# Two-layer decoder, cross attention: a ring of seven PSUM banks for the transposed scores, the denominators in one of its banks, and a semaphore of their own for them

## The reference, cut to what matters

```python
x = x + _L0_xattn_ref(_layernorm(x), ctx_1024, ctx_1024, ..., mask_SxS2_bk1, mask_BxS2_bf0)
...
q = (query @ Wq + bq).reshape(B, Sq, H, hd)
k = (key @ Wk + bk).reshape(B, Sk, H, hd)
v = (value @ Wv + bv).reshape(B, Sk, H, hd)
score = jnp.einsum('bqhd,bkhd->bhqk', q, k)
score = jnp.where(cmask, -jnp.inf, score)
att = jax.nn.softmax(score * scale, axis=-1)
ret = jnp.einsum('bhqk,bkhd->bqhd', att, v).reshape(B, Sq, D)
return ret @ Wo + bo
```

## Time and profile before

| | us |
|---|---|
| median of 3 runs | 1632.97 (1627.45 to 1636.53) |
| the profiled execution, device time | 1634.7 |
| its span, first to last instruction | 1632.8 |
| PE busy | 1401.2 (86%) |
| DVE busy | 1015.4 (62%) |
| ACT busy | 758.5 (46%) |
| share of the chain that ended last | PE 72%, DVE 14%, ACT 3% |
| mean granted TensorE clock | 0.921 of 2.4 GHz |

### The profile page before, as it was taken

One profiled execution on the slowest core, in us unless ns is written; L12 is line 12 of the kernel. 1 busy time (PEld: TensorE's weight loads), 2 busy tenths in 40 slices (PEclk: granted clock), 3 DMA queues, 4 the chain that ended last, 5 costly groups with the idle time before them and its releaser, 6 DMA issues.

```text
span 1632.8 us, 44292 instructions
## 1 busy us (share of the span) xinstructions
PE 1401.2 (86%) x17837; PEld 872.8 (53%) x17837; DVE 1015.4 (62%) x2607; ACT 758.5 (46%) x1942; POOL 236.9 (15%) x216
## 2 busy tenths in 40 slices
PE   5888888696499999999967989898989998889856
PEld 3343443393267676766643466445654565346545
DVE  3566656424477777877744677667766776777633
ACT  1313142251266666666632277235734474337534
POOL 2011121123030030110001200011001200030035
PEclk8989899797799999999987999899998999799969
DMA  9600000023230100100023000000000000000031
GB/s 320 244 16 0 16 1 7 17 60 99 77 144 4 24 22 10 36 3 16 4 55 69 1 1 2 3 14 1 2 3 14 1 2 1 1 14 2 1 88 53
DMA packets 56617, 59.09 MB, mean 36 GB/s; under 512 B 27853, under 2 KB 42064, under 8 KB 55264
## 3 DMA queue, kind: packets, MB, share of 16 engines
q1 hardware_dynamic: 53600, 50.97, 9.9%
q0 software_dynamic: 2528, 5.27, 1.0%
q10 hardware_dynamic: 288, 0.03, 0.0%
HBM read 32.56 MB, written 24.14 MB: 35 GB/s over the span
## 4 chain that ended last, share of the span: by engine, by line
PE 72%; DVE 14%; issue 4%; ACT 3%; SPq 2%; DMA 2%; POOL 2%; ACTq 0%; POOLq 0%; DVEq 0%
PE ps L1163 7%; PE ps L1551 6%; PE ps L1570 5%; PE ps L264 5%; PE ps L1143 4%; PE ps L1584 4%; PE ps L1153 4%; PE ps L1184 4%; DVE arena L610 4%; PE ps L1539 3%; PE ps L485 3%; PE ps L509 3%; PE ps L1198 2%; PE ps L1593 2%; PE ps L834 2%
## 5 line engine op out<-in xcount | busy, mean ns | idle before, releaser
L1296 DVE TENSOR_REDUCE nmax<-ps 128x1 f32<-128x512 f32 x256 | 166.7, 683 | 60.6 <-PE ps L1153 59.8
L1626 ACT ACTIVATE arena<-ps,arena 128x512 f32<-128x512 f32 (+3 forms) x256 | 135.3, 531 | 116.4 <-DVE arena L1689 109.2
L1689 DVE TENSOR_REDUCE arena<-ps 128x1 f32<-128x512 f32 (+3 forms) x256 | 124.3, 487 | 74.2 <-PE ps L1555 72.4
L1256 ACT ACTIVATE arena<-ps,nmax 128x512 f32<-128x512 f32 x172 | 118.8, 691 | 83.8 <-DVE nmax L1296 82.5
L1570 PE MATMUL ps<-sqc,arena 128*128 128x128 f32 x640 | 107.6, 290 | 20.3 <-DVE arena L1697 20.1
L1304 DVE COPY arena<-ps 128x512 f32<-128x512 f32 x128 | 88.0, 687 | 35.4 <-PE ps L1163 33.8
L264 PE MATMUL ps<-identb 128*128 128x512 bf16 x366 | 105.9, 453 | 1.4 <-DVE kcol L742 1.4
L610 DVE TENSOR_REDUCE arena<-ps 128x8 f32<-128x1232 f32 x64 | 89.0, 1437 | 29.1 <-PE ps L473 29.1
L1697 DVE TENSOR_SCALAR arena<-arena 128x512 f32<-128x512 f32 (+3 forms) x256 | 100.9, 394 | 9.1
L1551 PE MATMUL ps<-arena 64*128 64x384 f32 (+3 forms) x512 | 105.4, 490 | 0.0
L1584 PE MATMUL ps<-arena 128*64 128x128 f32 x1280 | 98.2, 284 | 0.0
(11 more groups left out here) (355 smaller groups left out, 2661.9 us busy)
## 6 DMA issues: line engine op xcount, KB each, us to landing
xs_d<-onehot SPq DMA_DIRECT2D x4, 2560.0 KB, 26.9
cw<-in_cw SPq DMA_DIRECT2D x2, 2048.0 KB, 11.0
rv<-in_rv SPq DMA_DIRECT2D x2, 1536.0 KB, 17.4
late<-in_gw SPq DMA_DIRECT2D x3, 1024.0 KB, 9.7
arena<-gs_d SPq DMA_DIRECT2D x23, 129.0 KB
onehot<-q_s SPq DMA_DIRECT2D x96, 8.0 KB
arena<-xs_d SPq DMA_DIRECT2D x23, 64.0 KB
xs_d<-arena SPq DMA_DIRECT2D x23, 64.0 KB, 1.6
```

What stands on the lines that cost most here:

```text
L1256: nc.scalar.activation(PB[k % 6], ps[:, k % 5, :], ACT.Exp, bias=nmax[:, u:u + 1], accum_out=rsum[:, b % 2, u:u + 1]).then_inc(SD["exp"], 1)
L1296: nc.vector.tensor_reduce(nmax[:, k % NU:k % NU + 1], ps[:, k % 5, :], AX.X, ALU.max, negate=True)\
L1626: nc.scalar.activation(TF["p%d" % (n % 2)][:, h * S:h * S + wd], ps[:, FSB[n % 2][h], 0:wd], ACT.Exp, bias=TF["nmax"][:, k4:k4 + 1], accum ...
L1689: nc.vector.tensor_reduce(TF["nmax"][:, k4:k4 + 1], ps[:, FSB[n % 2][h], 0:wd], AX.X, ALU.max, negate=True)\
```

## The change

The ring of transposed scores gets a seventh bank (`n % 7`), so tile n waits for the exponential of tile n - 7 and not of n - 6, and tile 6 waits for none. The output sum moves from bank 6 to bank 7, and the denominators from bank 7 to bank 6. Bank 6 is a bank of the ring, whose last tile in it is n = 13 (period 3). The last product of `sums()` raises a new semaphore, `sum`. DVE waits for `sum` ahead of the first reciprocal, and for the last count of `pv` only ahead of the first multiplication. No arithmetic is added or taken away.

```diff
-                "kv", ..., "st", "exp", "acc", "pv", "o")}
+                "kv", ..., "st", "exp", "acc", "sum", "pv", "o")}
+        NXP, XV, XS = 7, 7, 6
...
                     n = NG4 * j + g
-                    if n >= 6:
-                        pe.wait_ge(s["exp"], both(k, b) * NPER * NG4 + n - 5)
+                    if n >= NXP:
+                        pe.wait_ge(s["exp"], both(k, b) * NPER * NG4 + n - NXP + 1)
-                    nc.tensor.matmul(ps[:, n % 6, :], kbd[rows, j * P:(j + 1) * P], q_t[rows, :], ...
+                    nc.tensor.matmul(ps[:, n % NXP, :], kbd[rows, j * P:(j + 1) * P], q_t[rows, :], ...
...
-                    ins = nc.tensor.matmul(ps[cols, 6, :], vs[:, j, cols], TX[f"pt{j % 2}{g}"],
+                    ins = nc.tensor.matmul(ps[cols, XV, :], vs[:, j, cols], TX[f"pt{j % 2}{g}"],
...
-                        nc.tensor.matmul(ps[GR * g:GR * (g + 1), 7, :], vmask[:, j, :],
+                        ins = nc.tensor.matmul(ps[GR * g:GR * (g + 1), XS, :], vmask[:, j, :],
+                ins.then_inc(s["sum"], 1)
...
-            dve.wait_ge(s["pv"], both(k, b) * NPER + NPER)
+            dve.wait_ge(s["sum"], both(k, b) + 1)
-            landed = [ch.mark(nc.vector.reciprocal(r[:, part[0]], ps[:, 7, part[0]]))]
+            landed = [ch.mark(nc.vector.reciprocal(r[:, part[0]], ps[:, XS, part[0]]))]
             for i in range(NT):
...
                 ch.wait(landed[i])
-                nc.vector.tensor_tensor(aoT[:, part[i]], ps[:, 6, part[i]], r[:, part[i]], ALU.mult).then_inc(s["o"], 1)
+                if i == 0:
+                    dve.wait_ge(s["pv"], both(k, b) * NPER + NPER)
+                nc.vector.tensor_tensor(aoT[:, part[i]], ps[:, XV, part[i]], r[:, part[i]], ALU.mult).then_inc(s["o"], 1)
```

More of the change, by code:

```diff
@@ L215, in decoder @@
         XA["B"] = XA["E"] = {n: sem(f"s_x_{n}") for n in (
-                "kv", "kt", "vrep", "kbd", "vs", "qp", "qt", "mask", "sc", "top", "mt", "mT", "mTc", "st", "exp", "acc", "pv", "o")}
+                "kv", "kt", "vrep", "kbd", "vs", "qp", "qt", "mask", "sc", "top", "mt", "mT", "mTc", "st", "exp", "acc", "sum", "pv", "o")}
         NXH = 2 * NT
         NACC = (NPER - 2) * NG4
+        NXP, XV, XS = 7, 7, 6
         used[0] = 0
@@ L481, in keys @@
                     n = NG4 * j + g
-                    if n >= 6:
-                        pe.wait_ge(s["exp"], both(k, b) * NPER * NG4 + n - 5)
+                    if n >= NXP:
+                        pe.wait_ge(s["exp"], both(k, b) * NPER * NG4 + n - NXP + 1)
                     rows = slice(GR * g, GR * (g + 1))
-                    nc.tensor.matmul(ps[:, n % 6, :], kbd[rows, j * P:(j + 1) * P], q_t[rows, :], start=True, stop=False,
+                    nc.tensor.matmul(ps[:, n % NXP, :], kbd[rows, j * P:(j + 1) * P], q_t[rows, :], start=True, stop=False,
                                      skip_group_check=True, tile_position=(GR * g, 0))
@@ L490, in shift @@
                     rows = slice(GR * g, GR * (g + 1))
-                    nc.tensor.matmul(ps[:, (NG4 * j + g) % 6, :], sel[rows, j, :], mT[rows, :], start=False, stop=False,
+                    nc.tensor.matmul(ps[:, (NG4 * j + g) % NXP, :], sel[rows, j, :], mT[rows, :], start=False, stop=False,
                                      skip_group_check=True, tile_position=(GR * g, 0))
@@ L495, in hide @@
                 for g in range(NG4):
-                    o = ps[:, (NG4 * j + g) % 6, :]
+                    o = ps[:, (NG4 * j + g) % NXP, :]
                     if k == "B":
@@ L584, in act_X @@
                 act.wait_ge(s["st"], both(k, b) * NPER * NG4 + n + 1)
-                nc.scalar.activation(TX[f"pt{j % 2}{g}"], ps[:, n % 6, :], ACT.Exp, scale=scale,
+                nc.scalar.activation(TX[f"pt{j % 2}{g}"], ps[:, n % NXP, :], ACT.Exp, scale=scale,
                                      bias=kcol[:, b, j:j + 1] if k == "B" else pcol[:, j:j + 1]).then_inc(s["exp"], 1)
@@ L625, in dve_X @@
                         .then_inc(s["acc"], 1)
-            dve.wait_ge(s["pv"], both(k, b) * NPER + NPER)
+            dve.wait_ge(s["sum"], both(k, b) + 1)
             r = TX["r"]
             part = [slice(i * P, (i + 1) * P) for i in range(NT)]
-            landed = [ch.mark(nc.vector.reciprocal(r[:, part[0]], ps[:, 7, part[0]]))]
+            landed = [ch.mark(nc.vector.reciprocal(r[:, part[0]], ps[:, XS, part[0]]))]
             for i in range(NT):
                 if i + 1 < NT:
-                    landed.append(ch.mark(nc.vector.reciprocal(r[:, part[i + 1]], ps[:, 7, part[i + 1]])))
+                    landed.append(ch.mark(nc.vector.reciprocal(r[:, part[i + 1]], ps[:, XS, part[i + 1]])))
                 ch.wait(landed[i])
-                nc.vector.tensor_tensor(aoT[:, part[i]], ps[:, 6, part[i]], r[:, part[i]], ALU.mult).then_inc(s["o"], 1)
+                if i == 0:
+                    dve.wait_ge(s["pv"], both(k, b) * NPER + NPER)
+                nc.vector.tensor_tensor(aoT[:, part[i]], ps[:, XV, part[i]], r[:, part[i]], ALU.mult).then_inc(s["o"], 1)
             if k == "B":
```

## The result

The changed kernel takes 1615.26 us (median of 4 runs, 1611.95 to 1617.0), the kernel before beside it 1634.75. The measured ratio is 0.9858, with a 95% interval of 0.9823 to 0.9893; the quotient of the two medians is 0.988 and lies in it. Measured again on another occasion it was 0.9848 (0.9803 to 0.9892). The forecast was 1620.4 against 1632.97, a ratio of 0.992: the direction was right, the size (12.6 us) little more than half of what came (19.5 us by the medians, 23 by the ratio).

The account below looks back on a forecast made before the run. PE was taken to bound the kernel, with DVE at the attention's end. Reciprocals 6.6, the ring's first refill 3.6 and its later periods 2.4 us sum to 12.6, so 1632.97 becomes 1620.4, range 1613 to 1628.

Parts of the forecast that it names:

- What bounds each place: Cross attention: PE's own work or its wait for exponentials bounds each period; at the attention's end, DVE.
- E's first refill: Layer 1, tiles 4 to 7 while the ring fills: 0.58 us in two sequences, 0.29 in first and last.
- B's later periods: Layer 0, 12 periods of 3.25 us after the ring has filled: PE's own time, so no gain.
- The rival that B would gain: Layer 0's periods hang on the exponential: 1.6 us more, 1618.8, or 1617.4; chance 0.14 together with another rival.
- E's later periods: Layer 1 after the ring has filled: 0.28 us less in each of 7 periods, 2.0 us; period falls to 2.67.
- The price of the added wait: Extra wait instruction on DVE ahead of the reciprocals: 0.04 us per attention, from a range of 0 to 0.09.
- The failed step: Slow clock stretches stay fixed in time, so work moved into one runs at half speed and half the gain is left.
- the clock's own gain: Fillers after the attention keep the higher clock: 3.3 to 6.6 us more, 1614 to 1617; chance 0.14 with another rival.
- E's second period: Layer 1, second period of sequences two and three: 0.20 us gained in each, 0.4 together.
- the clock takes back half: Time saved ahead of slow clock stretches is worth half: 6.3 us left, 1626.7; chance 0.15.
- The ring does nothing: Another wait stands right behind the exponential, so only the reciprocals' 6.6 us are left: 1626.4; chance 0.07.
- Slower: Shifted attention ends open extra slow stretches in fillers and the stage behind; 12 make it 8 us slower, 1641; chance 0.04.

Follow-up runs that it names:

- the halves: The kernel before with only the early reciprocals (1619.63 us, ratio 0.989), and with only the ring of seven banks (1619.28 us, ratio 0.9886).
- the hole filled: Changed kernel plus ten filler products in PE's 2.6 us wait ahead of the first transposes of layer 1's last attention: 1604.56 us, ratio 0.9794.
- the delay: Kernel before plus one unused 128x512 copy on DVE ahead of the first reciprocal: 1645.49 us, ratio 1.0046.

## Why the prediction was right, and where it failed

*What bounds each place.* Right but for E's first refill, of which more below. B's later periods are PE's own work: 3.25 us with either ring, against the releaser that the trace names. On that place the rule of the Trainium skill ("TensorEngine Tiling (Array Packing)", Key Properties) that a change of tiling mode drains TensorE agrees with the trace: the 0.99 us from values to keys stayed with a bank more (70.93 to 71.92). The rival that B would gain is out. E's later periods lost 0.28 us each, and 2.67 us was the period to come. The reciprocals were ready 0.86 us earlier, and every one of the eight showed it.

*The price of the added wait.* I took 0.04 us per attention from a range of 0 to 0.09. It is nothing: the reciprocals moved by 0.86 and not by 0.82, and the multiplication stands 1.69 us behind them as before. No slower reciprocal either (0.96 us), so the bank next door costs nothing.

*The failed step* is the one that priced TensorE's clock. The sum took stretches at 1.2 GHz as fixed in time, so that in two of E's four attentions a saving ahead of them was worth half, and the rivals put the clock's own gain into the fillers, within a chance of 0.14. The attentions gave 22.0 us and not 12.6. Three things were wrong in it.

First, slow stretches aren't fixed in time. With six banks the wait in E's first refill prolongs one over the next period, by some 2.1 us there and 0.5 in the refill, in half of the attentions; with seven never. So E's second period, priced at 0.4 us, gave 4.2, and the first refill, priced at 1.7, gave 3.1. That sum hides two errors: 0.29 each for the first and last sequence were 1.74 and 0.82, and the whole 0.58 for the other two were 0.25 and 0.34. The trace of the kernel before had it: the fourth attention's periods of 4.10 and 4.96 us, at 0.50 of the clock from 1396 to 1410. I took it as circumstance and not as an effect of the wait. The Trainium skill ("TensorE: Matmul & The Clock Gate", A second HAM failure mode: psum-queue depth-cycling) says that small idle spells between groups of products, while cycling through PSUM banks, make the clock swing, and by it I should have given that rival more. The runs agree with it for E's first refill (6 of 8 against 0 of 4).

Second, the last projections ran at the lower level in most attentions (0.94 us) and don't now (0.57), 2.2 us that I had at zero.

Third, a reckoning that adds waits can't see what the clock does with a saving in the stages behind. A layer's sequences follow each other at distances that step by about 3.4 us. In layer 0 the two distances of 71.9 and 71.3 became 68.3 each, 6.6 us, of which 4.1 lie in the attentions. In layer 1 the last two, 170.6 and 170.4, became 167.3 each, 6.4 us, of which 4.6 lie in the attentions. In this pair of profiles the other stretches took as much back, so the total is the attentions' 22.0 less 1.9. The steps are needed for the totals of the halves, not for this sum.

*The rival "the clock takes back half"* was the opposite of what happened. *"The ring does nothing"* is out: alone it is worth 1.1%. *"Slower"* had its mechanism named rightly in one thing, that small shifts open or close slow stretches. The closing was the likely side. Against the kernel before beside it (0.9175 to 0.919), the clock was higher wherever waits were taken away: 0.9225 with early reciprocals in B, 0.930 with all of them, 0.929 with seven banks, 0.9275 with the change, 0.934 with the hole filled as well (medians over the runs). With the delay it was lower, 0.9155. But it doesn't grow with the waits taken away: the whole change has no higher clock than either half.

*The base.* I argued from an execution of 1634.7 us at clock 0.921, close to the median shown. Over all later runs the kernel before has a median of 1638.7 to 1640.5 at 0.9175 to 0.919, and the changed kernel measured beside it is 25.7 us faster by the medians, where the first occasion gave 19.5. The 12.6 us that I reckoned are half of that or a little more.

Open: the steps are PE's time at the lower clock, but what sets the step a layer settles on is not known. The attention's length alone doesn't (22.6 us at 170.6, 23.0 at 167.2), and no run told why the distances stand 3.4 us apart. The later waits put back alone gave 167.5, 170.7 and 167.2 in one execution, so they may matter to it too.

## What to carry to other kernels

Price a wait on TensorE's path twice: once by its length, and once by the clock of what runs behind it. In this kernel a microsecond of wait taken from the path or put into it was worth 1.4 to 3 in the total, and two edits that each removed waits didn't add. Where a trace shows work of the same kind at both clock levels, ask what the engine did just before the slow one. Row groups that idle during a wait can be filled with small products into a free bank, which took the slow period away here but moved the total by no more than the noise. A hole ahead of a long dense stage can be filled with full ones, which did pay here. And don't take the named releaser of a wait for granted: compare the gap with the same step at a place where that releaser came later.

## What the runs showed of the hardware that I had not expected

- Whether two tiles' keys wait for one exponential more (0.58 us each) while the other row groups work can decide at which clock the next period runs: 4.96 us in 6 of 8 attentions with the wait, 2.67 to 2.89 us in 4 of 4 without.
- Two small bf16 products on the idle row groups (0.39 and 0.60 us at the lower clock) remove this (8 of 8) without shortening any wait.
- Distances between equal stages settle on values about 3.4 us apart: 163.7 to 164.4, 166.9 to 167.3 and 170.4 to 170.9 us between the later sequences of layer 1, 68.1 to 68.7 and 70.6 to 71.9 in layer 0. They differ in PE's busy time on the same products (156.2 against 153.2 us) and hardly in its idle time.
- Ten useless products of 2.3 us in all, put into a hole, went with a program 10 us faster, 7 of them in the distances of the layer that has the hole.
